# A K/V tile of its own, an earlier x load, and no scores for masked queries, in an FFN–attention–FFN kernel on eight cores

## The chip, the cores and the metric

The kernel runs on the 8 cores of one Trainium2 chip (two dies of four cores). Each core works on a quarter of one of the two sequences; the cores exchange nothing. The metric is device time in microseconds, that of the slowest core, as the median of several runs.

## What is computed

```python
x = x + 0.5 * ffn(layernorm(x))
x = x + attn(layernorm(x))
x = x + 0.5 * ffn(layernorm(x))
# x: (2, 4096, 2048) float32

def attn(hs):                       # 16 heads, D = 128, latent L = 64
    Q = hs @ Wq.T; latent_k = hs @ Wk.T; latent_v = hs @ Wv.T
    q_latent = einsum('bthd,hdl->bthl', Q, q_to_latent)
    logits = einsum('bthl,bsl->bhts', q_latent, latent_k) / sqrt(L)
    # causal: keys j > i get -1e30; in the band i - 64 <= j <= i a further
    # 0.5 * (sum of q_latent) * (sum of latent_k) / sqrt(L) is added
    ctx = softmax(logits) @ (latent_v @ v_up)
    return ctx @ Wo.T

def ffn(x):                         # K = 8 experts of rank R = 64
    h = relu(x @ W1 + b1)
    alpha = softmax(h @ W2 + b2)
    return sum_k alpha_k * (x @ V_k.T) @ U_k.T
```

## The kernel before

A core owns 1024 query tokens: every fourth tile of 128 tokens of its sequence. It keeps activations transposed, features on the partitions, tokens on the free axis: `x_res` is 128 x (16 chunks x 1024 tokens) in float32. Waits are all written by hand. `ct`, `cs`, `cv` are counters of TensorE, ScalarE and VectorE; a wait names the count that it needs. Each engine and each DMA queue works in program order.

**Phase 1** (`for j in range(4)` in `build_fused`) computes K and V for the whole sequence, so it goes over four blocks of 1024 tokens, the core's own last. A round is:

1. four loads of `x_res`, 2 MB each, from the SP queue (L745 to L748). Each waits until the one before has landed (`dx`), and for a release `rel`.
2. LayerNorm 1 (`emit_ln`): for each of 16 chunks, ScalarE squares the chunk (L176) into one buffer, TensorE adds up the chunk over partitions (L183, L186) and its square (L190, L192). Then come short row operations, a matmul that spreads 1/sigma over the partitions (L230, L232), and 16 applies on VectorE (L242) that write `xhat`. TensorE and ScalarE wait for the last apply before they go on.
3. the FFN (`emit_ffn`): W1 in `emit_big_proj` (weights in four loads from GpSimd, 16 output tiles in two PSUM tiles in turn, L318), z = W2 h (L400), its copy (L410), eight transposes, a copy, softmax over 8 experts, the products with V (L512) and U (L570).
4. LayerNorm 2, of the same form; then the K/V product into `kv_ps` (L772, L779), its copy to `kvout` (L790) and two DMAs from GpSimd into `kaug` and `vt_sb`.

PSUM tiles are taken from a stack and given back at the end of a `with`. So `kv_ps` lies where the next LayerNorm's sums will lie, and the first load of round j+1, which lets that LayerNorm start, waits for the copy out of `kv_ps` (`kvs_tok`); the three others wait for the applies of chunks 7, 11 and 15 of LayerNorm 2, which read `x_res` last. `p_z` (two banks) and `p_ztr` (the transposes, part of a bank) are PSUM tiles of their own inside the FFN.

After phase 1 come the Wq projection and some setup for attention.

**Attention.** For each of 16 heads there are 32 key tiles of 128 keys. Key tile i sees queries from `qlo` = 128 * (i // 4) on; queries before it are masked. For tile i:

- `emit_outer(i)` and `emit_select(i)` on VectorE (L1341, L1401) make the mask and band term `mr`;
- `emit_scores(i)` on TensorE writes K.q into `PC` (L1383), in pieces cut at PSUM banks of 512 columns and at the end of the diagonal part;
- `emit_imm(i)` adds `mr` through an identity matmul (L1418);
- `emit_exp(i)` on ScalarE takes exp from PSUM (L1440), one instruction a bank;
- `emit_sums_ctx(i)` adds the row sums (L1459) and the context (L1462).

The loop over i issues on TensorE, in this order: a stage of the next head's preparation (`emit_A_stage`, in steps 2 to 15 and 26 to 33), `emit_imm(i-1)`, `emit_sums_ctx(i-2)`, `emit_scores(i)`. On VectorE a step is: that stage's row or copy operations, `emit_outer(i)`, `emit_select(i)`. `PC` has one buffer of two banks, so the first piece of a bank in `emit_scores(i)` waits for the exponential of tile i-1 in that bank.

Of the preparation the stages k = 4 to 11 (L1151, steps 6 to 13) find row maxima; k = 12 (step 14) transposes them (L1180), copies (L1189), writes them to DRAM (L1195) and reads them back as a row (L1205), both by DMA; k = 13 (step 15) waits for that row on VectorE (L1216, L1219). Head 15 prepares nothing.

For tiles 0 to 15 `PC` is addressed by the query itself (`dlt == 0`), and the pieces cover queries 0 to 1024:

```python
if dlt == 0:
    pieces = split_ranges(0, NTOK, (qlo, qlo + lead, 512))
else:
    pieces = split_ranges(qlo, NTOK, (qlo + lead,))
```

From tile 16 on they begin at `qlo`. `emit_exp` and `emit_sums_ctx` read from `qlo` on in all tiles.

**Phase 3** is the Wo projection, LayerNorm 3, the second FFN on the core's own tokens, and the store of the result.

Of the kernel before, what the change touches and what calls it, by code (L numbers as in the profile page):

```python
# [8 lines left out]
F32 = mybir.dt.float32  # L9
# [9 lines left out]
NTOK = 1024  # L19
# [327 lines left out]
def emit_ffn(nc, block, bufs, S, x_chunks, xhat, varr_dram, uarr_dram,  # L347
             rhs_ready=None, mrr=None, mr_tok=None, first=False):
    ct, cs, cv = S['ct'], S['cs'], S['cv']
# [29 lines left out]
    u = uid()  # L379
    with contextlib.ExitStack() as ps:  # L380
        P = [ps.enter_context(nc.psum_tensor(f"fe{u}_p{i}", [128, NTOK], F32))
             for i in range(2)]
        p_z = ps.enter_context(nc.psum_tensor(f"ffn_z{u}", [8, NTOK], F32))
        p_ztr = ps.enter_context(nc.psum_tensor(f"ffn_ztr{u}", [128, 64], F32))
        p_a8 = ps.enter_context(nc.psum_tensor(f"ffn_a8{u}", [8, NTOK], BF16))
# [9 lines left out]
        @block.tensor  # L395
        def _(t):
            w2v = bufs['w2_sb'].rearrange("p (k m) -> p k m", k=NCH)
            for k in range(NCH):
                for half in range(2):
                    mi = t.matmul(p_z[:, 512 * half:512 * half + 512],  # L400
                                  w2v[:, k, :],
                                  h_sb[:, NTOK * k + 512 * half:
                                       NTOK * k + 512 * half + 512],
                                  start=(k == 0), stop=(k == NCH - 1))
            mi.then_inc(ct.h, 1)
# [18 lines left out]
        def _(v):  # L424
            v.wait_ge(ct.h, ztr_tok)
            v.tensor_copy(zt[:, :], p_ztr[:, :]).then_inc(cv.h, 1)
        zt_tok = cv.inc()
        @block.vector
        def _(v):
# [204 lines left out]
def build_fused():  # L634
# [31 lines left out]
    with contextlib.ExitStack() as stx:  # L666
# [20 lines left out]
        with contextlib.ExitStack() as ph1:  # L687
# [44 lines left out]
            vt512 = vt_sb.rearrange("p (t c) -> p t c", c=512)  # L732
            kv512 = kvout.rearrange("p (t c) -> p t c", c=128)
            ln2_q = None
            kvs_tok = None
            for j in range(4):
                xq_toks = []
                for qd in range(4):
                    if ln2_q is None:
                        rel = wkvsum_tok if qd == 0 else None  # L740
                    else:
                        rel = kvs_tok if qd == 0 else ln2_q[4 * qd + 3]
                    @block.sync
                    def _(sy, j=j, qd=qd, rel=rel, dxn=dx.n):
                        sy.wait_ge(dx.h, dxn)  # L745
                        if rel is not None:
# [12 lines left out]
                                    mrr=mrr1, mr_tok=mr1,  # L759
                                    first=(j == 0))  # L760
                w2l = [(cv.h, res_toks[c]) for c in range(NCH)]
                _, ln2_q, mr2 = emit_ln(nc, block, bufs, S, x_chunks, xhat,
                                        wait0=w2l, mrr=mrr2)
                with nc.psum_tensor(f"kv_ps{j}", [128, NTOK], F32) as kv_ps:
                    @block.tensor
                    def _(t, mr2=mr2, ln2_q=ln2_q):
                        t.wait_ge(cv.h, mr2)
                        wv = wkv_sb.rearrange("p (k m) -> p k m", k=NCH)
                        for k in range(NCH):
# [17 lines left out]
                    def _(v, kv_tok=kv_tok, dn=dlat.n):  # L787
# [3 lines left out]
                                      kv_ps[:, :]).then_inc(cv.h, 1)  # L791
                    kvs_tok = cv.inc()
                @block.gpsimd
                def _(g, j=j, kvs_tok=kvs_tok):
# [31 lines left out]
        with contextlib.ExitStack() as attn_stack:  # L826
# [173 lines left out]
            with nc.psum_tensor("PA", [128, NTOK], F32) as PA, \  # L1000
# [322 lines left out]
                for h in range(H):  # L1323
# [25 lines left out]
                    def emit_scores(i, first_waits):  # L1349
# [5 lines left out]
                        def _(t, i=i, qlo=qlo, lead=lead, ql=ql, dlt=dlt):  # L1355
# [3 lines left out]
                            if dlt == 0:  # L1359
                                pieces = split_ranges(0, NTOK,  # L1360
                                                      (qlo, qlo + lead, 512))
                            else:
# [155 lines left out]
        with contextlib.ExitStack() as f2:  # L1518
# [11 lines left out]
            def wo_cb(m, pap, mm_tok):  # L1530
                @block.vector
                def _(v, m=m, pap=pap, mm_tok=mm_tok):
# [7 lines left out]
                extra_wait=(cv.h, ctxout_tok))  # L1540

            _, ln3_ap, mr3 = emit_ln(nc, block, bufs, S, x_chunks, xhat3,
                                     wait0=(cv.h, wo_last), mrr=mrr3)
            ffn2_res = emit_ffn(nc, block, bufs, S, x_chunks, xhat3,
                                dr['varr'], dr['uarr'],
                                rhs_ready=[(cv.h, t) for t in ln3_ap],
                                mrr=mrr3, mr_tok=mr3, first=True)
            @block.sync
# [85 lines left out]
```

## Time and profile before

| | |
|---|---|
| median of 3 runs | 3570.49 us (3570.41 to 3585.57) |
| the profiled execution | 3589.27 us, span of its slowest core (core 2) 3586.5 us |
| spans of the 8 cores | 3534.4 to 3586.5 us |
| mean granted clock of TensorE, per core | 0.742 to 0.758 of full speed |
| busy on core 2 | TensorE 2903.2 us (81%), VectorE 1118.8 (31%), ScalarE 698.1 (19%) |

The page and all views are of core 2 where no other core is named. Times in a timeline are from the start of the core's span. A matmul's duration runs to its modelled end, which overlaps the next one; how long it holds the engine is read from start to start. PEld is the weight load of TensorE, SPq the DMA queue of SP. A view shows in brackets how long the engine sat idle before an instruction, and what ended that.

### The profile page before, as it was taken

How to read it: one execution, taken by the hardware profiler on the slowest of the kernel's cores; microseconds unless marked ns; L12 is line 12 of the kernel's file. 1: busy time of each engine (PE TensorE's matmuls, PEld its weight loads, DVE VectorE, ACT ScalarE, POOL GpSimd, SP SyncE). 2: the span in 40 equal slices, each digit the busy share in tenths (PEclk: the TensorE clock that was granted, in tenths of full speed). 3: DMA queues.
4: the chain of work that ended last, by engine and by line, in shares of the span. 5: the costliest groups of instructions: out<-in, count | busy, mean ns of one | idle time of the engine just before them, and what ended most of it. 6: DMA issues, size and time to landing. Idle time of an engine off the chain costs nothing.

```text
span 3586.5 us, 32108 instructions; the slowest of 8 cores (3534.4 to 3586.5 us)
## 1 busy us (share of the span) xinstructions
PE 2903.2 (81%) x10766; PEld 1044.4 (29%) x10943; DVE 1118.8 (31%) x2081; ACT 698.1 (19%) x1149; POOL 51.3 (1%) x78
## 2 busy tenths in 40 slices
PE   4988578857885798495788888888888888888886
PEld 1432133312331233141232222222222232333332
DVE  2003320322032203212444444444444444311103
ACT  2101211121112110100232323232332232302010
POOL 0000000000000000000000000000000000000000
PEclk8999789978997899797555555555555555589898
DMA  4320243024302430221000000000000000040332
GB/s 127 68 47 0 97 71 71 0 97 71 71 0 97 71 71 0 50 47 27 3 1 1 1 1 1 1 1 1 1 1 1 1 1 1 1 94 3 74 65 94
DMA packets 14787, 128.17 MB, mean 36 GB/s; under 512 B 6369, under 2 KB 6682, under 8 KB 7562
## 3 DMA queue, kind: packets, MB, share of 16 engines
q0 software_dynamic: 6848, 82.28, 12.4%
q1 hardware_dynamic: 7786, 43.83, 3.4%
q8 instruction: 98, 1.61, 0.2%
q14 instruction: 55, 0.45, 0.0%
HBM read 196.53 MB, written 9.27 MB: 57 GB/s over the span
## 4 chain that ended last, share of the span: by engine, by line
PE 76%; DVE 11%; DMA 5%; issue 4%; ACT 3%; DVEq 0%; POOL 0%; ACTq 0%; SPq 0%; POOLq 0%
PE bp_p L318 22%; PE PC L1383 7%; PE PB L1459 7%; PE PD L1462 7%; PE fe_p L570 4%; DVE xhat L242 4%; PE fe_p L512 4%; PE ln_sum L183 4%; PE ln_sum L186 4%; PE PC L1418 3%; PE PA L1297 2%; PE PA L1248 2%; PE bp_p L331 1%; PE bp_cs L288 1%; ACT probs L1440 1%
## 5 line engine op out<-in xcount | busy, mean ns | idle before, releaser
L318 PE MATMUL bp_p<-xhat,wslotP 128*128 128x512 bf16 x2503 | 565.1, 383 | 63.7 <-DVE xhat L242 38.4
L1440 ACT ACTIVATE probs<-PC 128x512 bf16<-128x512 f32 (+3 forms) x768 | 352.7, 487 | 906.1 <-PE PC L1418 519.8
L1383 PE MATMUL PC<-qlat_h,kaug 65*128 65x256 bf16 (+3 forms) x1312 | 397.1, 423 | 39.2 <-ACT probs L1440 27.8
L1459 PE MATMUL PB<-probs,ones_bf 128*1 128x512 bf16 (+3 forms) x768 | 356.6, 464 | 19.1 <-ACT probs L1440 19.0
L318 PEld LDWEIGHTS bp_p<-xhat,wslotP 128*128 128x128 bf16 x2560 | 245.8, 99 | 383.3 <-issue 104.7
L1462 PE MATMUL PD<-probs,vexp 128*128 128x512 bf16 (+3 forms) x705 | 335.8, 476 | 0.0
L176 ACT ACTIVATE ln_sq<-x_res 128x1024 bf16<-128x1024 f32 x144 | 152.1, 1056 | 756.2 <-DVE x_res L580 313.0
L1401 DVE COPY_PREDICATED mr<-bandm_sb,ob 128x256 bf16<-128x256 uint8 (+1 forms) x512 | 210.7, 412 | 135.2 <-DVE ob L1341 62.4
L1418 PE MATMUL PC<-mr,ident_bf 128*128 128x256 bf16 (+1 forms) x576 | 194.5, 361 | 63.9 <-DVE mr L1401 61.3
L1383 PEld LDWEIGHTS PC<-qlat_h,kaug 65*128 65x128 bf16 x1312 | 162.0, 131 | 214.1 <-issue 209.3
L358 ACT ACTIVATE bbuf<-bp_p,b_sb 128x1024 bf16<-128x1024 f32 x80 | 89.1, 1114 | 673.8 <-PE bp_p L331 673.8
L183 PE MATMUL ln_sum<-x_res,ones_f 128*1 128x512 f32 x288 | 151.3, 607 | 54.3 <-DMA x_res<-xall 46.4
L242 DVE TENSOR_TENSOR xhat<-x_res,ln_rrep 128x1024 bf16<-128x1024 f32 x144 | 163.7, 1214 | 24.2 <-PE ln_rrep L232 24.2
L410 DVE TENSOR_SCALAR ffn_zsb<-ffn_z,b_sb 8x1024 f32<-8x1024 f32 x5 | 6.4, 1271 | 473.8 <-PE ffn_z L400 473.8
L186 PE MATMUL ln_sum<-x_res,ones_f 128*1 128x512 f32 x288 | 149.8, 602 | 0.0
L1462 PEld LDWEIGHTS PD<-probs,vexp 128*128 128x128 bf16 x768 | 78.6, 102 | 242.8 <-issue 227.9
L1341 DVE TENSOR_SCALAR ob<-qshrepb,ksumT 128x256 bf16<-128x256 bf16 (+1 forms) x512 | 139.9, 273 | 0.0
L1418 PEld LDWEIGHTS PC<-mr,ident_bf 128*128 128x128 bf16 x576 | 73.2, 129 | 201.9 <-issue 189.6
L318 PE MATMUL bp_p<-bbuf,wslotF 128*128 128x512 bf16 x501 | 111.8, 383 | 16.0 <-DMA wslotF<-woq 15.4
L570 PE MATMUL fe_p<-ffn_vx,wslotP 128*128 128x512 bf16 x500 | 117.8, 396 | 7.8 <-DVE ffn_vx L552 6.6
L1459 PEld LDWEIGHTS PB<-probs,ones_bf 128*1 128x1 bf16 x768 | 60.7, 79 | 217.7 <-issue 201.2
L199 DVE TENSOR_SCALAR ln_m<-ln_sum 1x1024 f32<-1x1024 f32 x9 | 10.9, 1211 | 362.0 <-PE ln_sq L192 362.0
(161 smaller groups left out, 2203.4 us busy)
## 6 DMA issues: line engine op xcount, KB each, us to landing
x_res<-xall SPq DMA_DIRECT2D x16, 2048.0 KB, 8.3
wslotP<-w1q POOLq DMA_DIRECT2D x16, 2048.0 KB, 16.3
wslotP<-varr POOLq DMA_DIRECT2D x4, 2048.0 KB, 14.9
wslotP<-uarr POOLq DMA_DIRECT2D x4, 2048.0 KB, 14.8
wslotP<-wqq POOLq DMA_DIRECT2D x4, 2048.0 KB, 15.5
wslotF<-woq POOLq DMA_DIRECT2D x4, 2048.0 KB, 12.5
wslotF<-w1q POOLq DMA_DIRECT2D x4, 2048.0 KB, 13.9
wslotF<-varr POOLq DMA_DIRECT2D x1, 2048.0 KB, 12.8
```

Of the source, the lines that this page charges most:

```text
L176: s.activation(sq2[par][:, :], src_chunks[c], AF.Square).then_inc(cs.h, 1)
L183: t.matmul(p_sum[:, 0:512], bufs['ones_f'][:, 0:1], src_chunks[c][:, 0:512], start=(c == 0), stop=(c == NCH - 1))
L186: t.matmul(p_sum[:, 512:1024], bufs['ones_f'][:, 0:1], src_chunks[c][:, 512:1024], start=(c == 0), stop=(c == NCH - 1))
L242: v.tensor_mul(dst[:, NTOK * c:NTOK * (c + 1)], src_chunks[c], p_rrep[:, :]).then_inc(cv.h, 1)
L318: mi = t.matmul(P[par][:, 512 * half:512 * half + 512], lhsT, rhs_sb[:, NTOK * k + 512 * half: NTOK * k + 512 * half + 512], start=(k == 0 ...
L570: mi = t.matmul(P[par][:, 512 * half:512 * half + 512], lhsT, vx[:, NTOK * j + 512 * half: NTOK * j + 512 * half + 512], start=(j == 0), s ...
L1383: mi = t.matmul(PC[:, a + dlt:b + dlt], kaug[0:65, 128 * i:128 * i + 128], ql[0:65, a:b], start=first, stop=stop)
L1401: v.copy_predicated(mr_sb[r][:, 0:lead], bandm_sb[:, 256 * r:256 * r + lead], ob_sb[i % 2][:, 0:lead]).then_inc(cv.h, 1)
L1418: mi = t.matmul(PC[:, a + dlt:b + dlt], bufs['ident_bf'][:, :], mr_sb[i % 4][:, a - qlo:b - qlo], start=False, stop=True)
L1440: s.activation(probs[i % 2][:, a:b], PC[:, a + dlt:b + dlt], AF.Exp).then_inc(cs.h, 1)
L1459: t.matmul(PB[:, a:b], bufs['ones_bf'][:, 0:1], probs[i % 2][:, a:b], start=(i == 0), stop=last)
L1462: mi = t.matmul(PD[:, a:b], vex[:, 128 * i:128 * i + 128], probs[i % 2][:, a:b], start=(i == 0), stop=last)
```

## The change

It has three parts. (1) `kv_ps` is taken once ahead of the round loop and held through phase 1, so the LayerNorms and FFNs use other banks. The first of the four x loads of rounds 1 to 3 waits for the apply of chunk 3 of LayerNorm 2 instead of the copy of K/V. (2) The FFN gets that tile as `zps` and puts z and, after z is copied out, its transposes there; the second FFN gets a tile `zps2`. TensorE now waits, ahead of z, for the last copy out of that tile (`prev_zt`, `prev_kvs`), and ahead of K/V for the last `prev_zt`. (3) In tiles 0 to 15 the scores are computed from `qlo` on.

```diff
 def emit_ffn(nc, block, bufs, S, x_chunks, xhat, varr_dram, uarr_dram,
-             rhs_ready=None, mrr=None, mr_tok=None, first=False):
+             rhs_ready=None, mrr=None, mr_tok=None, first=False, zps=None):
...
-        p_z = ps.enter_context(nc.psum_tensor(f"ffn_z{u}", [8, NTOK], F32))
-        p_ztr = ps.enter_context(nc.psum_tensor(f"ffn_ztr{u}", [128, 64], F32))
+        p_z = zps[0:8, :]
+        p_ztr = zps[0:128, 0:64]
...
         @block.tensor
-        def _(t):
+        def _(t, pzw=bufs.get('prev_zt', 0), pkv=bufs.get('prev_kvs', 0)):
+            t.wait_ge(cv.h, pzw)
+            t.wait_ge(cv.h, pkv)
...
         zt_tok = cv.inc()
+        bufs['prev_zt'] = zt_tok
...
+            kv_ps = ph1.enter_context(
+                nc.psum_tensor("kv_ps", [128, NTOK], F32))
             ln2_q = None
             kvs_tok = None
             for j in range(4):
...
-                        rel = kvs_tok if qd == 0 else ln2_q[4 * qd + 3]
+                        rel = ln2_q[4 * qd + 3]
...
-                                    first=(j == 0))
+                                    first=(j == 0), zps=kv_ps)
...
-                with nc.psum_tensor(f"kv_ps{j}", [128, NTOK], F32) as kv_ps:
+                if True:
                     @block.tensor
-                    def _(t, mr2=mr2, ln2_q=ln2_q):
+                    def _(t, mr2=mr2, ln2_q=ln2_q, pzw=bufs['prev_zt']):
                         t.wait_ge(cv.h, mr2)
+                        t.wait_ge(cv.h, pzw)
...
                     kvs_tok = cv.inc()
+                    bufs['prev_kvs'] = kvs_tok
...
                             if dlt == 0:
-                                pieces = split_ranges(0, NTOK,
-                                                      (qlo, qlo + lead, 512))
+                                pieces = split_ranges(qlo, NTOK,
+                                                      (qlo + lead, 512))
...
+            zps2 = f2.enter_context(
+                nc.psum_tensor("zps2", [128, NTOK], F32))
...
-                                mrr=mrr3, mr_tok=mr3, first=True)
+                                mrr=mrr3, mr_tok=mr3, first=True, zps=zps2)
```

## Rows read from the trace of the kernel before

**Rows 1.** The spans of the cores, with each core's mean granted clock.

```profile
core 1: 3536.7 us, clock 0.758
core 2: 3586.5 us, clock 0.742
```

**Rows 2.** The page, granted clock in 40 equal slices, tenths of full speed.

```profile
PEclk8999789978997899797555555555555555589898
```

**Rows 3.** Timeline at the first border between rounds: start, length, engine, line.

```profile
368.53 18.19 DVE L242 TENSOR_TENSOR xhat<-x_res,ln_rrep 128x1024 bf16<-128x1024 f32 x16 [2.68 <-PE ln_rrep L232]
...
396.14 0.60 PE L779 MATMUL kv_ps<-mrr,wkvsum 1*128 1x512 bf16 x2
...
398.22 26.72 SPq L748 DMA_DIRECT2D x_res<-xall  x4
...
408.81 1.86 PE L183 MATMUL ln_sum<-x_res,ones_f 128*1 128x512 f32 x2 [12.07 <-DMA x_res<-xall]
...
412.41 1.02 PE L183 MATMUL ln_sum<-x_res,ones_f 128*1 128x512 f32 x2
...
414.56 1.02 PE L183 MATMUL ln_sum<-x_res,ones_f 128*1 128x512 f32 x2
```

**Rows 4.** The same engine's timeline at the two later borders.

```profile
774.30 1.87 PE L183 MATMUL ln_sum<-x_res,ones_f 128*1 128x512 f32 x2 [12.32 <-DMA x_res<-xall]
...
1139.25 1.87 PE L183 MATMUL ln_sum<-x_res,ones_f 128*1 128x512 f32 x2 [12.05 <-DMA x_res<-xall]
```

**Rows 5.** The x loads (issue to landing) and the applies, by line, ns.

```profile
DMA to landing us min/median/max: 7.5/8.3/10.7
...
L242 DVE TENSOR_TENSOR xhat<-x_res,ln_rrep x144: 1212/1214/1222, 72.0 to 3332.2; 128x1024 bf16<-128x1024 f32 x144
```

**Rows 6.** Timeline in one head, key tiles 9 to 15.

```profile
2122.14 1.06 PE L1383 MATMUL PC<-qlat_h,kaug 65*128 65x512 bf16 x3
2123.00 0.42 PE L1151 MATMUL PA<-kwin_sb,qlat_h 66*128 66x256 bf16 x1
...
2131.02 1.06 PE L1383 MATMUL PC<-qlat_h,kaug 65*128 65x384 bf16 x4
2131.88 0.42 PE L1151 MATMUL PA<-kwin_sb,qlat_h 66*128 66x256 bf16 x1
...
2132.61 0.77 ACT L1440 ACTIVATE probs<-PC 128x128 bf16<-128x128 f32 x2 [2.52 <-PE PC L1418]
...
2133.72 0.43 DVE L1401 COPY_PREDICATED mr<-bandm_sb,ob 128x256 bf16<-128x256 uint8 x1 [0.17 <-DVE ob L1341]
2133.98 1.06 PE L1383 MATMUL PC<-qlat_h,kaug 65*128 65x384 bf16 x4 [0.33 <-issue]
2134.84 0.42 PE L1180 MATMUL PA<-ident_f,bmaxT 128*8 128x128 f32 x1
2135.05 0.42 PE L1418 MATMUL PC<-mr,ident_bf 128*128 128x128 bf16 x2
...
2139.26 1.06 PE L1383 MATMUL PC<-qlat_h,kaug 65*128 65x384 bf16 x4
2141.65 0.37 PE L1418 MATMUL PC<-mr,ident_bf 128*128 128x128 bf16 x2 [1.33 <-DVE mr L1401]
```

**Rows 7.** Groups by line and shape: busy us, mean ns, idle before and releaser.

```profile
L1418 PE MATMUL PC<-mr,ident_bf 128*128 128x128 bf16 x192 | 43.3, 295 | 25.9 <-DVE mr L1401 24.0
...
L1216 DVE TENSOR_TENSOR cfin<-cb_sb,bm_row 1x1024 f32<-1x1024 f32 x16 | 19.4, 1212 | 38.4 <-DMA bm_row<-crow_d 38.4
...
L400 PE MATMUL ffn_z<-bbuf,w_sb 128*8 128x512 bf16 x160 | 35.3, 379 | 6.8 <-ACT bbuf L358 6.8
```

**Rows 8.** Timeline of GpSimd, one instruction at the same place of each head.

```profile
2171.86 0.94 POOL L1066 MEMSET qlat_h<- 1x1024 bf16 x1 [89.39 <-PE PC L1383]
2259.11 0.94 POOL L1066 MEMSET qlat_h<- 1x1024 bf16 x1 [86.30 <-PE PC L1383]
2349.62 0.94 POOL L1066 MEMSET qlat_h<- 1x1024 bf16 x1 [89.57 <-PE PC L1383]
```

**Rows 9.** Stretch from step 2 of head 14 to the Wo projection, cores 2 and 1.

```profile
2977.90:3155.70 177.80, 148.05 (x472) 48.46 (x480) 64.06 (x167) 49.53 (x104) 1.09 (x2) 0.50 0.07 15
2953.10:3105.30 152.20, 122.55 (x480) 43.53 (x480) 64.06 (x167) 49.65 (x104) 1.09 (x2) 0.65 0.08 16
```

The columns of rows 9 are the stretch, its length, busy us and instructions of PE, PEld, DVE, ACT and POOL, the granted clock, the DMA share and GB/s.

## The prediction

> **What bounds the kernel now.** I read the spans of the eight cores first, because the metric is the slowest core and nothing ties the cores together: they end between 3534 and 3586 us, and the slow ones have the lower mean granted clock [rows 1]. The slice view of the page shows where that clock goes: TensorE is near full speed in the first 19 slices (four rounds of LayerNorm, FFN, LayerNorm, K/V projection) and near half, 1.2 GHz, in the 16 heads of attention [rows 2]. So a column of a matmul costs about twice as much in the heads as outside them.
>
> The timeline across the border between two rounds shows the first target. The last K/V matmul is issued at 396.14 us, the first load of the next x follows at 398.22, after the K/V copy, and TensorE stands still for 12.07 us until that load lands [rows 3]. The other two borders show 12.32 and 12.05 us [rows 4]. The second target is inside a head. There TensorE's timeline is closed: the scores, the mask product, the sums and the context follow each other without idle time in tiles 4 to 13, so TensorE sets the pace [rows 6]. One wait stands out, 1.33 us before the mask product of tile 15 [rows 6]; over the program such waits add up to 24.0 us on the 128-column form [rows 7].
>
> **Part 1, K/V gets a PSUM tile of its own; the first x load goes earlier.** Today the first load waits for the K/V copy, and the three others queue behind it on SP. After the change it waits for the fourth apply of LayerNorm 2. The 16 applies start at 368.53 and take 18.19 us [rows 3], 1.14 each from start to start, so it is released near 373.1. Four loads of 8.3 us in a row (26.72 us separate the first and last issue [rows 3], 10.7 is the slowest landing [rows 5]) land near 382, 391, 400 and 409; the releases of loads 2 to 4 (applies 8, 12, 16, up to 386.7) come before the load ahead has landed. LayerNorm 1 then starts when the K/V matmuls end, at about 396.8, and needs chunks 4, 8 and 12 at 405, 414 and 423. Each load is some 14 us early. What is late next is nothing: the loop over chunks is bound by TensorE itself, 2.15 us a chunk (412.41 to 414.56) [rows 3]. The square on ScalarE for chunk 0 needs only its load and moves under the K/V matmuls.
>
> The gain per border is the stall, plus the slow start behind it: the first chunk took 3.60 us (408.81 to 412.41), the later ones 2.15 [rows 3]. Part of the difference is the granted clock, low just after the pause; I count it as gained, 1.45 us. The sum is 12.07 + 12.32 + 12.05 = 36.4, plus 3 x 1.45 = 4.4, together 40.8 us. If the slow start stays it is 36.4.
>
> Cost: the three 2 MB groups of loads now run beside LayerNorm 2's applies and the K/V matmuls, which no row of before shows. The nearest rows: an apply took 1212 to 1222 ns in all 144 cases, 80 of them beside weight loads of LayerNorm 1's stage [rows 5], and the chunk loop kept 2.15 us while x loads ran [rows 3]. I take nothing; the other bound is in the rivals.
>
> **Part 2, z and its transpose share that tile.** Copies and waits between z, its copy, the transposes and their copy are already in the program, so the order on TensorE and VectorE stays. TensorE gets two waits in each of five FFNs and one before each of four K/V products, all on values reached long before (the last K/V copy, the last z copy). They stand in front of the z product, where TensorE waits for ScalarE anyway (6.8 us in five FFNs [rows 7]); I cost them at nothing, and at 14 x 0.05 = 0.7 us if nothing hid them. The five FFNs otherwise keep their order.
>
> **Part 3, the scores of masked queries go.** For key tiles 4 to 15 the program computes queries 0 to qlo and nobody reads them. Removed per head: 4 x 128 + 4 x 256 + 4 x 384 = 3072 columns in 12 matmuls. The price is by column, not by matmul: four pieces of tile 12 (1024 columns) occupy TensorE from 2131.02 to 2131.88, three pieces of tile 9 (also 1024 columns) from 2122.14 to 2123.00, 0.86 us both [rows 6]. That is 0.84 ns a column, so 2.58 us a head.
>
> Not all of it counts. The transpose of the row maxima (L1180, 2134.84) starts a chain for the next head: copy, two small DMAs through DRAM, then two row operations on VectorE, in front of which the selects queue. The select of tile 15 sits behind them on VectorE, and the mask product of tile 15 waits for it until 2141.65 [rows 6]; VectorE's wait for the second DMA is 38.4 us in 16 heads [rows 7]. These 6.81 us (2134.84 to 2141.65) do not shrink. The cuts of tiles 14 and 15 (768 columns, 0.65 us) lie inside it and only lengthen the 1.33 us wait. Tiles 4 to 13 keep 2304 x 0.84 = 1.94 us. Cover lost: in tile 12 the exponentials end at 2132.61 + 0.77 = 2133.38, while the next scores start at 2133.98; without the leading piece they are still ready. The select of tile 13 ends at 2133.72 + 0.43 = 2134.15 and is wanted at 2135.05 [rows 6]; one cut of 0.32 us lies between its start and there, so 0.58 us of room stay. So 15 heads x 1.94 + 2.58 in the last head, which prepares no next one, = 31.7 us.
>
> **The sum.** 40.8 + 31.7 = 72.5 us. The profiled execution took 3589.27 us (span 3586.5 and 2.8 around it), so 3517. It is slower than the median by 18.8 us, and the clock explains that: the median, taken bare, would give 3498. The difference between them is the largest open term.
>
> **What the clock does with it.** The same head of core 2 takes 87.25 us (2171.86 to 2259.11) and then 90.51 (2259.11 to 2349.62) [rows 8], since some heads hold stretches at 2.4 GHz and some none. From step 2 of head 14 to the Wo projection core 1 took 152.2 us at a mean clock of 0.65, core 2 177.8 us at 0.50, with the same instructions [rows 9]: core 1 got a long stretch at 2.4 GHz in the last head, core 2 none. Shorter heads start at other moments, so the stretches will fall differently, and I can't read from the rows which core gets them. Bounds: if core 2's alternate heads lose theirs, 7 x 3.26 = 23 us come back, 3540 on the profiled execution's time. If the slowest core gets the long one, 25.6 us go. Part 3 takes away matmuls without idle time and adds 0.65 us of pause per head, which speaks for somewhat fewer stretches; I give 17 of the median's 72.5 us back: 3570.5 - 72.5 + 17 = **3515 us**, near the 3517 of the profiled execution too.
>
> **Rivals.**
> - *The clock returns most of part 3.* Stretches at 2.4 GHz vanish from the heads or from the last head of the slowest core: 3540 as above, 3530 to 3552 with the last head. For: the clock is at half through nearly all of attention, so the stretches are marginal events [rows 2, 8]. Against: they sit also in cores with the same work and other phases. The Trainium skill, TensorE: Matmul & The Clock Gate, Part 1, says the low clock is the default and activity releases it; by that rule less work could mean fewer stretches, and the time would be this rival's. Chance 0.22.
> - *The clock goes the other way.* Every core gets the last head's stretch: 3570.5 - 72.5 = 3498 and down to 3485. Chance 0.15.
> - *The cut pieces were cover.* The exponential or select waits take their place as they do at tile 15, in all cut tiles: part 3 gives only the last head, 3570.5 - 40.8 - 2.6 = 3527. Against it is the room of 0.6 us. Chance 0.07.
> - *The early loads slow LayerNorm 2 (the other sign).* Each of 36 applies released beside a load, at 1.22 us, would have to cost 2.0 us more (72.5 / 36) before the kernel were slower; doubled applies cost 44 us and leave 3545 or so. The rows on loads beside other work speak against it [rows 3, 5]. The Trainium skill, SBUF — State Buffer, "two separate sides", says engine and DMA ports cannot contend; by that rule this rival has no chance at all, and the rows shown agree so far. Chance 0.03.
> - *The first load is not the stall's cause*, so the wait turns into one on a later quarter: part 1 gives under 10 us, 3545. Chance 0.03.
>
> **Numbers.** The forecast, both parts with some of the clock lost (3500 to 3530), has 0.50; the rivals 0.22, 0.15, 0.07, 0.03, 0.03. About 0.5% (18 us) is what a measurement of this kernel tells from no change: 3552.6 is its border. The range 3490 to 3542 leaves out the tail of the first two rivals and most of the last two, 2 in 10. Faster 0.94; same 0.05 (the clock rival's far end, the loads); slower 0.01.
>
> **What would show it.** Right: L183 idles for DMA only at the very start; its first chunk of rounds 2 to 4 takes near 2.2 us; x loads are issued under the applies, which stay at 1.21 us; L1383 has 192 records fewer; the wait of L1418 in tile 15 grows from 1.33 to about 2.0 us; heads without a fast stretch take 90.5 - 1.9 = 88.6 us. Wrong: a new wait of L183 on chunk 4, 8 or 12; scores that wait for exponentials in tiles 12 to 15; heads at 88.6 on all cores with no stretch among them, or a last head at 2.4 GHz on every core.

## The result and the profile after

The changed kernel took 3471.48 us (median of 10 runs), against 3590.36 for the kernel before in the same session. The ratio over comparable runs is 0.9706, with a 95% interval from 0.9671 to 0.9741; on the 3570.49 us of the table above that is 3465 us. The forecast was 3515 and its range began at 3490: the direction was right, the gain nearly twice as large as forecast (2.9% for 1.6%). Executions in which a die ran disturbed are left out of ratios, and so is the disturbed die of e9's profile (cores 0 to 3); where too few executions were left for a ratio, the stages of the profile are compared instead.

The profiled execution of after took 3479.84 us. First the spans of its cores, with the mean granted clock of each, against [rows 1].

```profile
core 0: 3477.5 us, clock 0.755
core 1: 3456.9 us, clock 0.764
core 2: 3445.6 us, clock 0.767
```

Core 2, the slowest before at 3586.5, is 140.9 us shorter, core 1 only 79.8. The slowest is now core 0, at the lowest clock of the eight. The slice view of the page, core 0, against [rows 2]:

```profile
PEclk8999889988998898797555555555555555698998
```

Attention is still near half. For core 2 the 140.9 us divide so, read from start to start of single matmuls: the three rounds of phase 1 from the last K/V product of round 1 to that of round 4 took 1095.8 us before and 1061.7 after (-34.1); round 1 and the setup up to step 2 of head 0 gain 6.5 more; the fourteen head lengths from step 2 of head 0 to step 2 of head 14 (heads are numbered 0 to 15) took 1237.4 and take 1161.6 (-75.8); from there to the Wo projection 177.8 and 152.0 (-25.8); the rest takes 1.4 longer. A forecast of 40.8 stands against the 34.1, one of 14 x 1.94 = 27.2 against the 75.8.

**The borders.** Timeline of core 2 of after at the first border, against [rows 3].

```profile
366.74 18.19 DVE L242 TENSOR_TENSOR xhat<-x_res,ln_rrep 128x1024 bf16<-128x1024 f32 x16 [2.69 <-PE ln_rrep L232]
371.44 24.67 SPq L753 DMA_DIRECT2D x_res<-xall  x4
385.08 1.06 ACT L176 ACTIVATE ln_sq<-x_res 128x1024 bf16<-128x1024 f32 x1 [22.34 <-DVE xhat L242]
...
394.32 0.60 PE L785 MATMUL kv_ps<-mrr,wkvsum 1*128 1x512 bf16 x2
394.85 1.02 PE L183 MATMUL ln_sum<-x_res,ones_f 128*1 128x512 f32 x2
397.00 1.02 PE L183 MATMUL ln_sum<-x_res,ones_f 128*1 128x512 f32 x2
399.15 1.02 PE L183 MATMUL ln_sum<-x_res,ones_f 128*1 128x512 f32 x2
```

The loads begin 4.7 us after the first apply, the square of chunk 0 has moved under the K/V product, and LayerNorm 1's sums follow K/V in 0.53 us. The first chunk takes 2.15 us like the others. The two groups by line say the same for the whole program: one DMA wait of L183 is left (at the very start), and the applies beside the loads take what they took in [rows 5].

```profile
  DMA x_res<-xall: 9.4, 1
...
L242 DVE TENSOR_TENSOR xhat<-x_res,ln_rrep x144: 1212/1214/1223, 70.8 to 3190.1; 128x1024 bf16<-128x1024 f32 x144
```

That is 13.6 us a border, as forecast: 12.1 to 12.4 of stall and 1.3 to 1.5 of slow start. But rounds 2 to 4 are shorter by 10.6, 10.1 and 13.5 only. What comes back lies mostly between the z product and the first product with U. Two stretches of core 2 of before, in rounds 2 and 3 (columns as in [rows 9]):

```profile
599.40:656.80 57.40, 42.41 (x189) 17.39 (x193) 13.94 (x23) 1.64 (x8) 0.00 (x0) 0.89 0.20 37
964.70:1022.10 57.40, 42.43 (x190) 17.44 (x194) 13.94 (x23) 1.64 (x8) 0.00 (x0) 0.89 0.20 37
```

and the same two of after:

```profile
584.10:643.50 59.40, 44.36 (x190) 17.83 (x194) 13.95 (x23) 1.64 (x8) 0.00 (x0) 0.84 0.19 36
938.90:999.20 60.30, 45.32 (x190) 17.93 (x194) 13.94 (x23) 1.64 (x8) 0.00 (x0) 0.84 0.19 35
```

The work of VectorE and ScalarE is the same, TensorE's busy time grows, its clock is lower: 2.0 and 2.9 us go back to the clock. In round 4 both kernels have 0.85 there, and nothing comes back.

**Inside a head.** Timeline of core 2 of after, key tiles 12 to 15, against [rows 6].

```profile
2060.09 0.42 PE L1158 MATMUL PA<-kwin_sb,qlat_h 66*128 66x256 bf16 x1
2062.20 0.74 PE L1390 MATMUL PC<-qlat_h,kaug 65*128 65x128 bf16 x3
2062.73 0.42 PE L1158 MATMUL PA<-kwin_sb,qlat_h 66*128 66x256 bf16 x1
2064.84 0.74 PE L1390 MATMUL PC<-qlat_h,kaug 65*128 65x128 bf16 x3 [0.33 <-issue]
2065.37 0.42 PE L1187 MATMUL PA<-ident_f,bmaxT 128*8 128x128 f32 x1
2069.48 0.74 PE L1390 MATMUL PC<-qlat_h,kaug 65*128 65x128 bf16 x3
2072.20 0.37 PE L1425 MATMUL PC<-mr,ident_bf 128*128 128x128 bf16 x2 [1.98 <-DVE mr L1408]
```

The scores of tile 12 hold TensorE for 0.53 us (2062.20 to 2062.73) where they held it for 0.86. No exponential or select is late in tile 12 or 13. From the transpose of the row maxima to the mask product of tile 15 it is 6.83 us, before 6.81, and the wait there has grown from 1.33 to 1.98 us, by the 0.65 us that tiles 14 and 15 were said to be worth.

The lengths of heads are in the timeline of GpSimd, against [rows 8]; core 2 of after:

```profile
1934.88 0.94 POOL L1073 MEMSET qlat_h<- 1x1024 bf16 x1 [81.22 <-PE PC L1390]
2016.60 0.94 POOL L1073 MEMSET qlat_h<- 1x1024 bf16 x1 [80.78 <-PE PC L1390]
2098.53 0.94 POOL L1073 MEMSET qlat_h<- 1x1024 bf16 x1 [80.99 <-PE PC L1390]
```

81.72 and 81.93 us, where before alternated between 87.25 and 90.51. The windows of the head from 2027.7 on show why:

```profile
2027.70:2031.10 3.40, 2.93 (x8) 0.75 (x9) 1.95 (x3) 1.20 (x2) 0.00 (x0) 0.50 0.00 0
2031.10:2037.90 6.80, 5.25 (x22) 1.54 (x20) 3.03 (x7) 4.22 (x6) 0.00 (x0) 1.00 0.01 2
2037.90:2078.90 41.00, 38.25 (x121) 12.34 (x122) 20.74 (x54) 12.17 (x28) 0.00 (x0) 0.50 0.00 1
2078.90:2085.70 6.80, 5.14 (x26) 2.09 (x26) 1.92 (x5) 3.37 (x7) 0.00 (x0) 1.00 0.00 0
2085.70:2109.60 23.90, 18.46 (x79) 6.80 (x78) 14.35 (x33) 5.59 (x13) 0.94 (x1) 0.50 0.00 1
```

Two stretches of 6.8 us at 2.4 GHz, at the same two places in nearly every head of most cores. Core 0 lacks the first in heads 0 to 11 (the second is there, some 4 us later in the head). Its first place:

```profile
2045.80:2052.60 6.80, 6.80 (x18) 1.34 (x16) 3.01 (x7) 1.72 (x3) 0.00 (x0) 0.50 0.01 2
```

At 2.4 GHz 22 matmuls are recorded in this place, at 1.2 GHz 18. On core 2 TensorE is through early and then waits for an exponential, 1.55 us where core 0 waits 0.59:

```profile
2037.66 0.95 PE L1390 MATMUL PC<-qlat_h,kaug 65*128 65x512 bf16 x3 [1.55 <-ACT probs L1447]
```

Over all eight cores, 112 heads of after fall into these, by rounded length: 82 to 83 us, 72 heads (two stretches); 84 to 85 us, 24 heads (most with one stretch, nine of core 0's among them); 86 to 87 us, 13 heads (most with one, three with only 3.4 us at 2.4 GHz); 88 us, three (3.4 us). No head is wholly at 1.2 GHz, so the forecast 88.6 us for such a head can't be read; its 1.9 us can, in the part from step 2 to the transpose of the row maxima: without a stretch in it, it took 42.17 us before and 40.26 after. The first stretch is worth 40.26 - 37.64 = 2.6 us in that part and 85.3 - 81.9 = 3.4 us in the whole head, half its length. This is where core 0's time goes: its fourteen heads took 1193.0 us, those of the other seven 1159 to 1170.

### The profile page after: what moved, and what is told of

The parts are those of the page before. It is cut to its first block, busy times and chain, and to the rows that moved or that the text cites. A ratio compares the mean times of both kernels' runs of the same rounds, so it can differ in the third digit from the quotient of the medians.

```text
span 3477.5 us, 31819 instructions; the slowest of 8 cores (3443.1 to 3477.5 us)
## 1 busy us (share of the span) xinstructions
PE 2853.2 (82%) x10719; PEld 1006.1 (29%) x10719; DVE 1118.8 (32%) x2081; ACT 698.1 (20%) x1149; POOL 51.3 (1%) x78
## 4 chain that ended last, share of the span: by engine, by line
PE 78%; DVE 12%; issue 3%; ACT 3%; DMA 3%; DVEq 0%; POOL 0%; ACTq 0%; SPq 0%; POOLq 0%
PE bp_p L318 23%; PE PD L1469 8%; PE PB L1466 7%; PE PC L1390 6%; DVE xhat L242 5%; PE fe_p L573 4%; PE fe_p L515 4%; PE ln_sum L183 4%; PE ln_sum L186 4%; PE PC L1425 3%; PE PA L1255 2%; PE bp_p L331 1%; PE PA L1304 1%; PE bp_cs L288 1%; PE kv_ps L778 1%
## 5 line engine op out<-in xcount | busy, mean ns | idle before, releaser
L318 PE MATMUL bp_p<-xhat,wslotP 128*128 128x512 bf16 x2560 | 574.5, 383 | 56.3 <-DVE xhat L242 56.3
L1469 PE MATMUL PD<-probs,vexp 128*128 128x512 bf16 (+3 forms) x768 | 363.6, 473 | 0.0
L1466 PE MATMUL PB<-probs,ones_bf 128*1 128x512 bf16 (+3 forms) x768 | 349.8, 456 | 12.4 <-ACT probs L1447 12.2
L1390 PE MATMUL PC<-qlat_h,kaug 65*128 65x256 bf16 (+3 forms) x1088 | 333.5, 407 | 17.6 <-ACT probs L1447 17.4
L1425 PE MATMUL PC<-mr,ident_bf 128*128 128x256 bf16 (+1 forms) x576 | 188.1, 349 | 87.1 <-DVE mr L1408 84.8
L1390 PEld LDWEIGHTS PC<-qlat_h,kaug 65*128 65x128 bf16 x1088 | 128.6, 124 | 167.1 <-issue 159.4
L183 PE MATMUL ln_sum<-x_res,ones_f 128*1 128x512 f32 x288 | 148.0, 596 | 16.3 <-DMA x_res<-xall 8.4
L515 PE MATMUL fe_p<-xhat,wslotP 128*128 128x512 bf16 x512 | 118.4, 391 | 0.9 <-DVE vsum L498 0.9
## 6 DMA issues: line engine op xcount, KB each, us to landing
wslotF<-woq POOLq DMA_DIRECT2D x4, 2048.0 KB, 13.3
```

The lines of the kernel that those rows point to most:

```text
L183: t.matmul(p_sum[:, 0:512], bufs['ones_f'][:, 0:1], src_chunks[c][:, 0:512], start=(c == 0), stop=(c == NCH - 1))
L318: mi = t.matmul(P[par][:, 512 * half:512 * half + 512], lhsT, rhs_sb[:, NTOK * k + 512 * half: NTOK * k + 512 * half + 512], start=(k == 0 ...
L515: mi = t.matmul(P[par][:, 512 * half:512 * half + 512], lhsT, xhat[:, NTOK * k + 512 * half: NTOK * k + 512 * half + 512], start=(k == 0), ...
L1390: mi = t.matmul(PC[:, a + dlt:b + dlt], kaug[0:65, 128 * i:128 * i + 128], ql[0:65, a:b], start=first, stop=stop)
L1425: mi = t.matmul(PC[:, a + dlt:b + dlt], bufs['ident_bf'][:, :], mr_sb[i % 4][:, a - qlo:b - qlo], start=False, stop=True)
L1466: t.matmul(PB[:, a:b], bufs['ones_bf'][:, 0:1], probs[i % 2][:, a:b], start=(i == 0), stop=last)
```

## The experiments

The table gives medians over the eight cores of each profile (cores 4 to 7 for e9), in us. Rounds 2 to 4 and the 14 heads are the stretches named above (in brackets the cores' extremes where they matter), "last" is the one behind them up to the Wo projection, "at 2.4" is TensorE's time at 2.4 GHz from step 2 of head 0 to the Wo projection. Each column is a median of its own, so rows needn't add up.

| kernel | rounds 2-4 | 14 heads | last | at 2.4 | ratio to before, 95% |
|---|---|---|---|---|---|
| before | 1095.8 (1095.4-1102.6) | 1230.9 (1217.6-1237.6) | 152.3 (to 178.8) | 146.8 | |
| after | 1061.7 (1061.7-1064.8) | 1161.1 (1159.3-1193.0) | 151.4 (to 156.5) | 201.4 | 0.9706 [0.9671, 0.9741] |
| e1_tile_and_load | 1061.7 | 1231.4 | 153.8 (to 177.6) | 143.4 | 0.9882 [0.9826, 0.9938] |
| e2_scores_only | 1095.8 | 1158.1 | 150.1 (to 167.7) | 215.0 | 0.9759 [0.9706, 0.9811] |
| e7_late_load | 1064.7 (1061.7-1065.1) | 1159.3 | 151.3 | 215.0 | none |
| e8_load_after_kv | 1102.3 (1095.5-1105.7) | 1157.8 | 153.1 (to 169.9) | 213.3 | none |
| e3_keep_14_15 | 1061.7 | 1156.3 | 151.0 | 215.0 | none |
| e4_keep_4_7 | 1061.7 | 1176.2 | 151.0 | 191.2 | 0.9711 [0.9654, 0.9768] |
| e6_keep_12_13 | 1061.7 | 1190.3 | 152.4 | 175.8 | none |
| e5_keep_8_11 | 1064.7 | 1197.1 | 154.5 (to 168.7) | 175.8 | none |
| e11_after_pause | 1061.7 | 1194.9 | 154.1 | 184.3 | none |
| e9_after_k13_at_18 | 1063.2 | 1147.8 | 149.6 | 174.1 | 0.9643 [0.9581, 0.9706] |
| e10_before_k13_at_18 | 1095.8 | 1216.0 (1213.1-1227.5) | 156.6 (to 172.9) | 117.8 | 0.9948 [0.9924, 0.9972] |

Four kernels have the same heads (after, e2, e7, e8). Their medians lie between 1157.8 and 1161.1 us, and between 201.4 and 215.0 us at 2.4 GHz; that is the spread against which the others are to be read.

**The parts alone.** e1 is after with the old scores (parts 1 and 2), e2 is before with the new ones (part 3).

```diff
# e1, on after
-                                pieces = split_ranges(qlo, NTOK,
-                                                      (qlo + lead, 512))
+                                pieces = split_ranges(0, NTOK,
+                                                      (qlo, qlo + lead, 512))
```

> Parts 1 and 2 alone, scores as before. Theory (each part acts alone, the clock's stretches depend on the length of a head): the three borders lose their stall, L183 starts 0.3 us after the K/V product, rounds 2 to 4 shrink by 10 to 14 us each as in the changed kernel, 32 to 40 us in all; heads keep their 85 to 90.5 us, since no head is shorter; ratio 0.989 to 0.991. Rival (the earlier loads or the other PSUM banks also speed up attention, so that the extra gain over the forecast comes from here): heads near 82 us, 80 to 110 us faster, ratio 0.97 to 0.977.

> Part 3 alone, K/V tile and loads as before. Theory: nearly all cores lock into heads of 82 us with two stretches at 2.4 GHz in each, although the cold part of a head shrinks by only 1.9 us; phase 1 as before with its 12 us stalls; 60 to 80 us faster, ratio 0.978 to 0.983. Rival (work alone, 31.7 us): heads near 86 to 88.6, ratio 0.991.

e1 took 3551.74 us (median), e2 3507.85, with 3588.17 for before beside them. Rounds 2 to 4 follow parts 1 and 2 alone (-34.1 us), the heads follow part 3 alone (-72.8), and neither touches the other's stage. The windows of the fourteen heads on core 4, before and e2:

```profile
1734.20:2971.80 1237.60, 1088.38 (x3684) 364.42 (x3740) 587.85 (x1414) 371.78 (x756) 13.23 (x14) 0.54 0.00 1
```

```profile
1730.80:2887.10 1156.30, 1007.57 (x3544) 330.10 (x3544) 587.81 (x1414) 371.66 (x756) 13.23 (x14) 0.58 0.00 1
```

VectorE and ScalarE do the same; PE has fewer records, and its clock is higher. Of the 69.8 us that after gains in the median core's fourteen heads, 14 x 1.91 = 27 are work (1.91 is what the part from step 2 to the transpose lost where it held no stretch, 42.17 - 40.26), 43 are clock. This also kills a sentence of the prediction, that the stretches fall anew because heads start at other moments. On core 4 the heads of e1 start 35 us before those of the kernel before, and the fourteen take 1231.4 and 1230.9 us in the median; in e2 and e8 they start 24 to 44 us later than in after and e7, and all four take 1157.8 to 1161.1. So the sum over fourteen heads follows the head's program and not its starting time. Single cores still differ under one program: core 0 of after, and the last stretch on cores 2, 4 and 6 of before (178 us, the others 152), on core 1 of e2 (167.7) and on cores 3 and 7 of e8 (167.9 and 169.9).

**Part 1 taken apart.** e7 releases all loads by the last apply, e8 the first by the K/V copy again, with the tile of its own kept.

```diff
# e7, on after
-                        rel = ln2_q[4 * qd + 3]
+                        rel = ln2_q[15] if qd == 0 else None
# e8, on after
-                        rel = ln2_q[4 * qd + 3]
+                        rel = kvs_tok if qd == 0 else ln2_q[4 * qd + 3]
```

> The changed kernel, but the first x load of rounds 1 to 3 released by the last apply of LayerNorm 2 (13.6 us later) instead of the fourth. It lands 8 to 10 us after the last apply; the K/V product takes 9 us from there. Theory: it is just in time or 0 to 2 us late, and the three later loads, 8.5 us apart, keep ahead of four chunks of 8.6 us; rounds 2 to 4 (1061.7 us) grow by 0 to 6 us in all. Rival (loads need the lead of 14 us): L183 waits on later chunks too, 15 us or more.

> The changed kernel with the first x load released by the K/V copy again, the K/V and z tile of its own kept. If the early load alone carries part 1, rounds 2 to 4 go back from 1061.7 to 1095 us and L183 waits 12 us at each border; the tile of its own is worth nothing by itself. Rival: the separate banks carry part of it, and the rounds stay below 1088 us.

Timeline of e7, core 0, at the first border:

```profile
365.27 18.18 DVE L242 TENSOR_TENSOR xhat<-x_res,ln_rrep 128x1024 bf16<-128x1024 f32 x16 [2.68 <-PE ln_rrep L232]
...
383.53 17.15 SPq L753 DMA_DIRECT2D x_res<-xall  x3
...
393.41 1.02 PE L183 MATMUL ln_sum<-x_res,ones_f 128*1 128x512 f32 x2
```

Loads issued 12 us later than in after still end before the sums want them on this core; on four others some come late, by 1.2 to 3.1 us in all. Rounds 2 to 4 are 3.0 us longer in the median: 1061.7 on three cores, 1064.7 to 1065.1 on five, where after has 1061.7 on six and 1064.8 on two. Core 0 is one of the five and has no wait for a late load, so not all of the 3.0 is the delay's. Timeline of e8, core 2:

```profile
394.63 1.23 DVE L796 CAST kvout<-kv_ps 128x1024 bf16<-128x1024 f32 x1 [10.23 <-PE kv_ps L785]
395.94 9.38 SPq L753 DMA_DIRECT2D x_res<-xall  x2
...
405.00 1.87 PE L183 MATMUL ln_sum<-x_res,ones_f 128*1 128x512 f32 x2 [10.54 <-DMA x_res<-xall]
```

The stall is back behind the copy, although nothing in PSUM asks for it, and rounds 2 to 4 take 1102.3 us, 6.5 more than before. So the tile by itself is worth nothing, and the early load is the whole of part 1. The 6.5 us are two longer rounds in the median core: in both kernels a round takes either 365 or 368.5 us, and e8 has 14 long ones of 24, before 4. Why e8 has more stays open. Whether the early load needs the tile was not tested. Without it LayerNorm 1's sums would have to wait for the K/V copy. By [rows 3] that is over some 2 us after the last K/V product (396.14 to 398.22), so an early load with the old tile might cost 2 us a border where before costs 12, an estimate.

**How the heads answer to a little work.** e3, e4, e6 and e5 give back the unread scores of some tiles: 14 and 15, 4 to 7, 12 and 13, 8 to 11.

```diff
# e3, on after; e4: 4 <= i <= 7; e6: i in (12, 13); e5: 8 <= i <= 11
+                                lo0 = 0 if i in (14, 15) else qlo
-                                pieces = split_ranges(qlo, NTOK,
-                                                      (qlo + lead, 512))
+                                pieces = split_ranges(lo0, NTOK,
+                                                      (qlo, qlo + lead, 512))
```

> The changed kernel with the leading score pieces of tiles 14 and 15 put back (768 columns a head). Theory (they lie inside the fixed chain of DMAs before the mask product of tile 15): heads keep their length, that wait falls from 2.0 to 1.35 us, time within 3 us of the changed kernel. Rival (each cut column counts): 0.65 us a head, 10 us more than the changed kernel, or more if the shorter wait changes the clock's stretches.

> The changed kernel with the leading pieces of tiles 4 to 7 put back (512 columns, 0.43 us a head). Work alone: 16 x 0.43 = 7 us more than the changed kernel. Clock theory: a head's length with both stretches was 81.9 to 82.3 us, the same in head after head; 0.43 us more may throw heads off the moments at which the stretches come, and then heads of 85 to 88 us are seen and the loss is 20 to 50 us, not 7.

> The changed kernel with the leading pieces of tiles 12 and 13 put back (768 columns, 0.64 us a head). Work alone: 14 heads 1170 us instead of 1161. Clock theory: between the 1176 seen with 0.43 us put back and the 1197 with 0.86, about 1185, with the time at 2.4 GHz between 176 and 191 us.

> The changed kernel with the leading score pieces of tiles 8 to 11 put back (1024 columns, 0.86 us a head). Work alone: the 14 heads of a core between the second and the last, 1161 us in the changed kernel, become 1173. Clock theory, after putting back 512 columns cost 15 us there instead of 6: fewer heads at 82 us, most at 85 and above, the 14 heads take 1185 to 1200 us, and the time spent at 2.4 GHz falls from 200 us towards 160.

e3 tests the claim that tiles 14 and 15 are swallowed. The group of mask products of 128 columns on core 4, in e3, and then in after:

```profile
L1426 PE MATMUL PC<-mr,ident_bf 128*128 128x128 bf16 x192 | 42.8, 291 | 25.6 <-DVE mr L1409 23.4
```

```profile
L1425 PE MATMUL PC<-mr,ident_bf 128*128 128x128 bf16 x192 | 42.8, 291 | 35.7 <-DVE mr L1408 33.9
```

With the columns back the wait falls to 23.4, near the 24.0 of [rows 7], and the heads are not longer (1156.3 for 1161.1, where a change within 3 us was expected): the columns stand where the pause stood. e4 gives back 512 columns at 0.84 ns, 0.43 us a head, 6.0 in fourteen, and costs 15.1 us. e6 gives back 768 columns, 9.0 us, and costs 29.2. e5, 1024 columns, 12.0 us, costs 36.0. Windows of the fourteen heads of e5, core 4:

```profile
1708.70:2903.00 1194.30, 1045.34 (x3599) 343.61 (x3598) 587.75 (x1414) 371.49 (x756) 13.23 (x14) 0.56 0.00 1
```

Each microsecond of work is answered by 1.5 to 2.2 of lost clock, and 2.4 GHz time falls from 201.4 to 191.2, 175.8 and 175.8 us. The expectation for e4 was a loss of 20 to 50 us or 7, and it is 15; e6 was expected near 1185 us; the fall towards 160 us that was expected of e5 did not come.

**Is it TensorE's work, or the length of the head?** e11 gives TensorE nothing to do. It repeats the maximum at the end of the chain in step 15, which writes the same values again, so the mask product of tile 15 waits longer.

```diff
# e11, on after, stage k = 13
...
                                          bm_row[:, :]).then_inc(cv.h, 1)
                             v.wait_ge(cv.h, cv.n + 1)
+                            v.tensor_max(cfin[:, :], cb_sb[:, :],
+                                         bm_row[:, :]).then_inc(cv.h, 1)
+                            v.wait_ge(cv.h, cv.n + 2)
...
-                        cv.inc(1)
+                        cv.inc(2)
```

> The changed kernel with one row maximum repeated on VectorE in stage k = 13 (same result), 1.22 us more in the chain before the mask product of tile 15; TensorE's columns are those of the changed kernel. Work alone: 14 x 1.25 = 17 us more in the 14 heads, 1178. Clock theory: the head is longer than the 82 us that repeated, some heads lose a stretch at 2.4 GHz, 14 heads take 1190 us or more with the same columns, and the time at 2.4 GHz falls below 180 us.

Both groups by form, and the windows of the fourteen heads, are of core 4.

```profile
L1226 DVE TENSOR_TENSOR cfin<-cb_sb,bm_row 1x1024 f32<-1x1024 f32 x16 | 19.4, 1213 | 2.4 <-DVE cfin L1223 0.9
...
L1428 PE MATMUL PC<-mr,ident_bf 128*128 128x128 bf16 x192 | 42.7, 290 | 58.9 <-DVE mr L1411 57.4
```

```profile
1707.30:2907.10 1199.80, 1033.01 (x3543) 332.43 (x3542) 604.60 (x1428) 371.55 (x756) 13.22 (x14) 0.56 0.00 1
```

The pause is there (57.4 us in the program, 33.9 on the same core of after). The maximum takes 1.213 us, and the stretch from the transpose to the mask product of tile 15 grows from 6.84 to 8.14 us (medians of the heads, core 4): 18 us in fourteen heads. They are 33.8 us longer. Each microsecond of waiting is answered by 0.9 of lost clock, less than the 1.5 to 2.2 of added columns but of the same sign (time at 2.4 GHz is 184.3 us; below 180 was expected). So a loss of clock needs no added column; a longer head is enough.

**A still shorter head.** The last stage of the preparation moves from step 15 to step 18, behind work that doesn't need it, on after (e9) and on before (e10).

```diff
-                            if 2 <= i <= 15:
+                            if 2 <= i <= 14:
                                 emit_A_stage(h + 1, i - 2)
+                            elif i == 18:
+                                emit_A_stage(h + 1, 13)
```

> The changed kernel with stage k = 13 of the next head's preparation moved from step 15 to step 18, so that VectorE no longer sits in front of the selects waiting for the second DMA. Not one column less on TensorE. Work: the 2.0 us wait of L1425 in tile 15 goes, a head without a fast stretch is 86.6 us instead of 88.6, 14 heads 28 us less, if the clock's stretches stay: 1133 us. Clock theory: the length of a head moves away from the 82 us at which they repeated, so the gain may be anything from 28 us down to a loss; the heads' lengths spread over several values.

> The kernel before with the same move of k = 13, scores as before. It shortens the head's part at 1.2 GHz by 1.33 us and removes no column. If removing columns is what made the heads of the changed kernel so short, 14 heads fall by 19 us (1231 to 1212). If it is the length of the head that decides when the stretches at 2.4 GHz fall, the fall differs clearly from 19 us, and the time at 2.4 GHz (147 us before) changes with it.

The wait of tile 15, e9 on core 4 and e10 on core 2:

```profile
L1425 PE MATMUL PC<-mr,ident_bf 128*128 128x128 bf16 x192 | 43.6, 295 | 4.6 <-DVE mr L1408 2.8
```

```profile
L1418 PE MATMUL PC<-mr,ident_bf 128*128 128x128 bf16 x192 | 43.5, 295 | 4.8 <-DVE mr L1401 2.6
```

It is gone in both: 14 x 1.98 = 28 us of the fourteen heads for e9, 14 x 1.33 = 19 for e10. The heads became shorter by 13.3 and 14.9 us. Here the clock takes back instead of giving, and 2.4 GHz time falls by 27.3 and 29.0 us. For e10 the 14.9 is only 4 us from the 19 that work alone would give. Heads of e9 (GpSimd, core 4) no longer repeat one length; three lengths follow each other in turn:

```profile
2019.37 0.94 POOL L1073 MEMSET qlat_h<- 1x1024 bf16 x1 [81.64 <-PE PC L1390]
2099.26 0.94 POOL L1073 MEMSET qlat_h<- 1x1024 bf16 x1 [78.94 <-PE PC L1390]
2182.38 0.94 POOL L1073 MEMSET qlat_h<- 1x1024 bf16 x1 [82.18 <-PE PC L1390]
2265.04 0.94 POOL L1073 MEMSET qlat_h<- 1x1024 bf16 x1 [81.72 <-PE PC L1390]
```

That is 79.9, 83.1 and 82.7 us. Measured from step 2 to step 2, this group comes back on cores 4 to 7 (about 245.6 us for three heads), as pairs of 87.1 and 90.4 us do on cores 2, 4 and 6 of before (177.5 for two) and 81.9 us alone does in after.

e9 is the best kernel here by its ratio, 0.9643 for 0.9706, though the intervals overlap. In its profile the four cores of die 1 end between 3432 and 3445 us, where those of after end between 3443 and 3459.

## Why the prediction was wrong

**Part 1, mis-sized by 7 us.** The stall and the slow start went as worked out, 13.6 us a border; the row of before on the loads' neighbours was a fair guide, since the applies kept 1.21 us. The Trainium skill, SBUF — State Buffer, "two separate sides", says that engine ports and DMA ports cannot contend, and these applies agree. Measured are 34.1 us of 40.8: 4.9 of the missing 6.7 are the lower clock behind z in rounds 2 and 3, the rest is spread over the rounds. That a removed pause changes the clock of a later stretch was not in the sum.

**Part 2, right.** The z product's wait for ScalarE, 6.8 us in [rows 7], is 7.9 after (6.3 in four FFNs, 1.6 in the fifth), and no new wait of TensorE shows at z, its transposes or K/V. No run has part 2 by itself; e1 and e8 put no price on it that could be told from nothing.

**Part 3, right as work.** 1.94 us a head was forecast, 1.91 measured; tiles 14 and 15 are swallowed by the chain, shown by the trace (the 0.65 us moved into the wait) and by e3. The cover held in tiles 12 and 13. The 2.58 us of the last head can't be told apart: the stretch behind the fourteen heads holds 1.94 + 2.58 us of cut columns at 1.2 GHz and fell by 0.9 us in the median core.

**"What the clock does with it", wrong, and with the wrong sign.** This is the step that failed. The prediction let the clock take back 17 us; it gave 43 in the fourteen heads of the median core (49 on core 2), and in the last stretch of core 2, which set the end before, some 21 more (25.8 less the 4.5 of cut columns). The bound on this side was the last head alone. The rows could have given a second one: [rows 8] hold heads of 87.25 and 90.51 us with the same instructions, so a stretch in every head instead of every second would have been worth 7 x 3.26 = 23 us, as much as was counted on the other side. The prediction took that bound for a loss only. The trace of before held the bound that was needed, on core 2 itself. One of its heads has two whole stretches of 6.8 us, at 3.4 and 54.6 us after step 2:

```profile
2526.85 0.94 POOL L1066 MEMSET qlat_h<- 1x1024 bf16 x1 [89.35 <-PE PC L1383]
2612.17 0.94 POOL L1066 MEMSET qlat_h<- 1x1024 bf16 x1 [84.37 <-PE PC L1383]
```

That is 85.3 us, and cores 1, 3 and 7 have several such heads. Fourteen like it would be worth 1237.4 - 14 x 85.3 = 43 us on core 2, near what came.

The reason given, less work without idle time means fewer stretches, is refuted for this cut: after has less work, more pause and 55 us more at 2.4 GHz. The rule of the Trainium skill, TensorE: Matmul & The Clock Gate, Part 1, that activity releases the clock was read as "more work, more clock"; no run here bears that out. e4, e6 and e5 add work and lose clock, e11 adds a pause and loses clock as well. e9 and e10 remove a pause and lose clock too.

**The rivals.** "The clock goes the other way" came nearest: the last head is at 2.4 GHz for part of its length on every core of after's profile (149.3 to 156.5 us, before up to 178.8). But it ended at 3485 because it priced that head alone, and e2 and e8 still have cores at 168 to 170 us there. "The clock returns most of part 3" did not happen. The cut pieces were no cover, the loads slow nothing, and the first load was the stall's cause (e8).

**What stays open.** What rule places the stretches. Length alone is not it: by the work in them, heads of e6 and e10 without a stretch would be about equally long (some 89.2 us, an estimate from the 90.5 of before and the work and waits moved), yet fourteen take 1190.3 and 1216.0 us. Their columns and pauses lie at other places of the head. It is also open why core 0 of after keeps one stretch a head while seven cores with the same program keep two; the profiles of e2, e7 and e8 have no such core (at most 1168.5 us in the fourteen heads), so it may differ from execution to execution.

## What to carry to other kernels

Where the slices of the page show TensorE near 1.2 GHz with short stretches at 2.4, cut the sum in two: the work removed, which the rows gave to a few per cent in the heads and a sixth too high in phase 1 (34.1 for 40.8), and the clock, whose two ends are "every repetition gets the best one seen on any core" and "none gets any". Look for the best repetition in the whole trace, on every core: here it stood in the slowest core's own trace. A small cut or wait in a body that is repeated sixteen times paid or cost here between half of its size (e9) and three times (e6), and only a run told which. And a buffer of its own is worth what is issued earlier because of it: ask which transfer it lets go, and by how much too early that transfer already is (here 12 us later cost 3 at most).

## What the runs showed of the hardware that was not expected

- The stretches at 2.4 GHz repeat in place and length: 6.8 us, starting 3.4 and 51.2 us after step 2, head after head, on most cores, which exchange nothing. Four kernels with the same heads (after, e2, e7, e8) agree in their fourteen heads within 3.3 us in the median. Where lengths of heads repeat, they do so in a fixed order: one length in after, two in turn on the slow cores of before, three in turn in e9.
- A pause of 1.3 us a head, made on VectorE, cost 33.8 us in fourteen heads, some 16 of them beyond the pause itself.
- A stretch of 6.8 us at 2.4 GHz is worth 2.6 to 3.4 us in after, not 6.8: at 1.2 GHz that place holds 18 matmuls, at 2.4 GHz 22, and behind them TensorE waits 1.55 us for ScalarE, where it waits 0.59 at 1.2 GHz.
- With 12 us of pause gone ahead of LayerNorm 1, the clock 190 us later, behind the z product, was 0.84 instead of 0.89 in rounds 2 and 3, and 0.85 in both kernels in round 4.
